# VectorE takes a group's residual behind the next group's locals, and TensorE turns x1 behind the cross matmuls

## The chip, the core and the metric

The kernel runs on one core of a Trainium2 chip. A core has five engines that work side by side, each with a queue of its own that it takes in order: TensorE (PE; its weight loads, PEld, overlap its matmuls), VectorE (DVE), ScalarE (ACT), GpSimd (POOL) and SyncE (SP, which issues the DMAs here). They wait for each other by semaphores. The metric is the time of one execution in device microseconds; the time of the kernel before is the median of three.

## The reference

32 batch rows of 128 tokens with 128 channels go through two layers, both with a residual. All is float32.

```python
# first layer (a gated trace layer), x: [32, 128, 128]
ctx    = causal_ema(x, tau_ctx)
wg     = sigmoid(concat([x, ctx]) @ Wg.T + bg)
gated  = x * wg
h1     = gelu(x @ Wn1.T + bn1)
mod    = 0.5 + sigmoid(h1 @ Wn2.T + bn2)                 # [b, t, 32]
traces = vmap(lambda tau, m: causal_ema(gated * m[..., None], tau))(tau_raws, mod)
temporal = einsum('dbtc,dc->btc', traces, softmax(blend, axis=0))
gate   = sigmoid(temporal @ Wtemp.T + btemp)
soma   = gelu(x @ Wsoma.T + bsoma)
out    = (soma * gate) @ Wout.T
x1     = x + (out - mean(out)) / sqrt(var(out) + 1e-5) * gamma + beta
# second layer: attention of 16 heads over 128 tokens; each batch row takes a dense or a
# sparse form by a threshold on exp(-5 * u_prev), then the output projection
q, k, v = x1 @ Wq.T + bq, x1 @ Wk.T + bk, x1 @ Wv.T + bv
y = x1 + attention(q, k, v, prior_indices, prior_mask, lam) @ Wo.T + bo
```

## The kernel before, in words

The 32 batch rows are 8 groups of 4 (`GB`); a group's tiles are 128 x 512. The first layer is a pipeline over the groups, in which every engine runs the same `step(i, m)`: it opens group m + 1 (functions `f_*`: context, gate, modulation, the eight lag products), finishes the traces of group m (`b_*`: carries, locals, cross, gate, output, moments) and closes group m - 1 (`c_*`: residual, q, k, v). There are seven steps; three are written out and four run in a loop of two turns, and all but the first close a group, so six do. After them `end()` works off the last group among the first attention rows, and `over_octets` does the attention (softmax over scores, two halves of 8 heads a batch row).

The order in each queue is written by hand. What matters around the change:

- VectorE: `b_carries` (three L1156, from PSUM to `bh`), `c_residual` of group m - 1 (four L1215: x1 = centred output times rstd plus xb), `f_gated` of group m + 1 (L1114, waits for ScalarE's tanh), `b_locals` (four L1165), `f_modulation` (L1120, L1121, L1124, L1126, L1128: the modulation and its split into bfloat16 parts `mod_pa` and `mod_pb`, each in SBUF), `b_temporal` (L1172, needs the turned cross), then the lag products (L1140, seven of L1144), with the rest of groups m and m - 1 between them.
- TensorE: local matmuls (L504, need the carries), `f_modulation` (L436), `c_x1T` (four transposes of x1, L385), `f_gated` (four transposes of the gated x, L385 too), `b_cross` (L515, need VectorE's locals), `f_modulation_n` (L446), `c_q` (L554, needs x1T on SBUF), `b_crossT` (L385, needs ScalarE's copy of cross), `c_k` (L557), then the lag matmuls (L470, L471; the first pair needs `mod_part3`, which VectorE's L1128 sets).
- ScalarE: the tanh of the gate (L811), of the modulation (L821), the copies of x1T (L854), of the turned gated x (L834), of cross (L839) and of the small modulation (L826).
- GpSimd: `f_inputs` of group m + 1 (L1386: xb = x + beta, waits for x1 of group m - 1), `c_keep` of m - 1 (L1418: x1 + bo), the decay products (L1393: three, then one; they need L826), the sums of lag products (L1406) and rstd (L1412). A load of x on SyncE's queue waits for xb.

`arena` is one large SBUF tensor that holds nearly all tiles; `ps` is PSUM. A row of the profile that reads `arena<-arena` has its tile operands in SBUF, one that reads `arena<-ps,arena` has one in PSUM.

Of the kernel before, what the change touches and what calls it, by code (L numbers as in the profile page):

```python
# [82 lines left out]
def build(nc, x, w, wn2, cols, rows, consts, ident_in, idx, masks, out):  # L83
    with ExitStack() as ctx:
# [156 lines left out]
        def at_start(i, m, before):  # L241

            return isinstance(i, int) and 2 * i + m < before
# [128 lines left out]
        def _(pe):  # L372
# [56 lines left out]
            def f_modulation(i, m):  # L429

                u = m % 2
                pe.wait_ge(s["h1_ready"], grp(i, m, 1, 1))
                if at_start(i, m, 1):
                    pe.wait_ge(s["vec_step"], vec(f"wn2_row{GB - 1}"))
                for b in range(GB):
                    mm = pe.matmul(bank(u, 1)[:, b * P:b * P + P], wn2_row[:, b, :], h1T[u], start=True, stop=True)  # L436
                mm.then_inc(s["modT_ps"], 1)
# [11 lines left out]
            def f_gated(i, m):  # L449

                u = m % 2
                pe.wait_ge(s["gated_ready"], grp(i, m, 1, 1))
                turned(bank(u, 2), gT[u], "gn_ps")
# [54 lines left out]
            def b_cross(i, m):  # L508

                u = m % 2  # L510
                pe.wait_ge(s["bh_ready"], grp(i, m, NJ + NCAR, NJ + NCAR))
                for j in range(NJ):

                    k = P if j else NLOC * D
                    mm = pe.matmul(bank(u, 0)[D * j:D * j + D, :], decay_p[0:k, :], bh[u][0:k, j, :],  # L515
                                   start=True, stop=True)
                mm.then_inc(s["cross_ps"], 1)
# [74 lines left out]
            def step(i, m):  # L592
                f_x(i, m + 1)
                f_context(i, m + 1)
                b_carries(i, m)
                f_soma(i, m + 1)
                f_gate(i, m + 1)
                f_hidden(i, m + 1)
                b_locals(i, m)
                f_modulation(i, m + 1)  # L600
                if not at_start(i, m, 1):
                    c_x1T(i, m - 1)
                f_gated(i, m + 1)
                b_cross(i, m)
                f_modulation_n(i, m + 1)
                if not at_start(i, m, 1):
                    c_q(i, m - 1)
                b_crossT(i, m)
                if not at_start(i, m, 1):
                    c_k(i, m - 1)  # L610
                f_lags(i, m + 1, range(0, 2))
                if not at_start(i, m, 1):
                    c_less(i, m - 1, 0, 0)
                b_gate(i, m)
                if not at_start(i, m, 1):
                    c_less(i, m - 1, 1, 0)
                f_lags(i, m + 1, range(2, 4))
                if not at_start(i, m, 1):
                    c_less(i, m - 1, 0, 1)
                f_lags(i, m + 1, range(4, 6))  # L620
                if not at_start(i, m, 1):
                    c_less(i, m - 1, 1, 1)
                    c_v(i, m - 1)
                b_out(i, m)
                f_lags(i, m + 1, range(6, Q))
                if at_start(i, m, 1):

                    pe.wait_ge(s["vec_step"], vec(f"hot{K_SPARSE - 1}"))
                    for j in range(K_SPARSE):
                        mm = pe.matmul(bank(1, 3)[:, 0:P], ident_b[:], one_hot[:, j, :],  # L630
                                       start=(j == 0), stop=(j == K_SPARSE - 1))
                    mm.then_inc(s["counts_ps"], 1)
# [147 lines left out]
        def _(act):  # L780
# [37 lines left out]
            def f_modulation(i, m):  # L818
                u = m % 2
                act.wait_ge(s["modT_ps"], grp(i, m, 1, 1))  # L820
                act.activation(thd[u], bank(u, 1), ACT.Tanh, bias=hb[:, 2:3], scale=0.5).then_inc(s["modT_tanh"], 1)  # L821
# [9 lines left out]
            def f_gated(i, m):  # L831
                u = m % 2
                act.wait_ge(s["gn_ps"], grp(i, m, 1, 1))
                act.activation(gn[u], bank(u, 2), ACT.Copy).then_inc(s["gn_ready"], 1)  # L834

            def b_cross(i, m):
                u = m % 2
                act.wait_ge(s["cross_ps"], grp(i, m, 1, 1))
                act.activation(crn[u], bank(u, 0), ACT.Copy).then_inc(s["cross_ready"], 1)  # L839
# [57 lines left out]
            def step(i, m):  # L897
                f_x(i, m + 1)
                f_context(i, m + 1)
                f_soma(i, m + 1)  # L900
                f_gate(i, m + 1)
                f_hidden(i, m + 1)
                f_modulation(i, m + 1)
                if not at_start(i, m, 1):
                    c_x1T(i, m - 1)
                f_gated(i, m + 1)
                b_cross(i, m)
                f_modulation_n(i, m + 1)
                if not at_start(i, m, 1):
                    c_parts(i, m - 1, 0)  # L910
                    c_part(i, m - 1, 0, 1)
                b_gate(i, m)
                if not at_start(i, m, 1):
                    c_part(i, m - 1, 1, 1)
                    c_parts(i, m - 1, 2)
                if at_start(i, m, 2) and m == 1:

                    act.wait_ge(s["vec_step"], vec("cnt_one"))
                    act.activation(lncnt[:], cnt1[:], ACT.Ln).then_inc(s["lncnt_ready"], 1)
# [85 lines left out]
        def _(dve):  # L1005
# [153 lines left out]
            def b_locals(i, m):  # L1159

                u = m % 2
                dve.wait_ge(s["local_ps"], grp(i, m, 1, 1))
                rows_of = slice(0, NLOC * D)
                for j in range(NJ):
                    dve.tensor_tensor(by_row(bh[u][rows_of, j, :]), by_row(bank(u, j)[rows_of, :]),  # L1165
                                      each_row_of(rows_of), ALU.mult).then_inc(s["bh_ready"], 1)
# [37 lines left out]
            def c_residual(i, m):  # L1204

                u = m % 2
                dve.wait_ge(s["rstd_ready"], grp(i, m, 1, 1))
                dve.wait_ge(s["xb_ready"], grp(i, m, 1, 1))
                dve.wait_ge(s["centred"], grp(i, m, GB, GB))
                if not at_start(i, m, 2):  # L1210

                    dve.wait_ge(s["x1b_ready"], grp(i, m, 1, 0))
                for b in range(GB):
                    cs = slice(b * P, b * P + P)
                    ins = dve.scalar_tensor_tensor(x1g[u][:, cs], ln[u][:, cs], rstd[:, u, b:b + 1], xb[u][:, cs],  # L1215
                                                   ALU.mult, ALU.add)
                ins.then_inc(s["x1_ready"], 1)
# [15 lines left out]
            def step(i, m):  # L1233
                closes, counts = not at_start(i, m, 1), at_start(i, m, 1)
                b_carries(i, m)
                if closes:
                    c_residual(i, m - 1)
                if counts:
                    neighbours()
                    one_hots(0, 8)  # L1240
                f_gated(i, m + 1)
                b_locals(i, m)
                if counts:
                    one_hots(8, 12)
                f_modulation(i, m + 1)
                b_temporal(i, m)
                if counts:
                    one_hots(12, 16)
                f_lags(i, m + 1, range(0, 2))
                if counts:  # L1250
                    one_hots(16, 20)
                f_lags(i, m + 1, range(2, 3))
                if counts:
                    one_hots(20, 24)
                f_lags(i, m + 1, range(3, 4))
                if counts:
                    one_hots(24, 28)
                b_mixed(i, m)
                f_lags(i, m + 1, range(4, 5))
                if counts:  # L1260
                    one_hots(28, K_SPARSE)
                f_lags(i, m + 1, range(5, 6))
                if closes:
                    c_values(i, m - 1)
                f_lags(i, m + 1, range(6, 7))
                c_moments(i, m)
                f_lags(i, m + 1, range(7, Q))
                c_centre(i, m)
                if counts:
                    late_tables()  # L1270
                if at_start(i, m, 2) and m == 1:

                    dve.wait_ge(s["lncnt_ready"], 1)
                    dve.tensor_tensor(neg_lc[:], count_none[:], lncnt[:], ALU.subtract).then_inc(s["neg_lc_ready"], 1)
# [274 lines left out]
```

## Time and profile before

| | us |
|---|---|
| median of three executions | 354.29 |
| lowest, highest | 354.13, 356.16 |
| profiled execution, whole | 355.99 |
| its span | 354.2 |

| engine | busy us | share of the span |
|---|---|---|
| PE | 316.7 | 89% |
| PEld | 216.5 | 61% |
| DVE | 293.7 | 83% |
| POOL | 232.6 | 66% |
| ACT | 212.5 | 60% |

The span runs from the first to the last instruction of the profiled execution; its whole time has 1.8 us around it. Busy shares are means over the two stages. In the views that follow, "idle before" is the time for which an engine stood still in front of an instruction, with what released it; where it stands at 0 or is missing the engine came straight from other work.

### The profile page before, as it was taken

The numbers are of one execution on the slowest core, as the hardware profiler recorded it, in microseconds if no ns is written. First come the engines' busy times: TensorE is split into PE (matmuls) and PEld (weight loads), VectorE is DVE, ScalarE is ACT, GpSimd is POOL, SyncE is SP. The second block draws the span as 40 slices with busy tenths as digits, with TensorE's granted clock in tenths as the row PEclk, the third lists the DMA queues.
The fourth block names the chain that finished last, engine by engine and source line by source line (L and its number), as shares of the span: only waits on it lengthen the run. The fifth ranks groups of instructions, "written<-read, shape, count | busy, mean of one in ns | idle before, by whom it ended". The sixth has DMA issues, their size and how long they took to land. (4 is left out here: it accounts for less than half of the span.)

```text
span 354.2 us, 10381 instructions
## 1 busy us (share of the span) xinstructions
PE 316.7 (89%) x3371; PEld 216.5 (61%) x3383; DVE 293.7 (83%) x1530; ACT 212.5 (60%) x452; POOL 232.6 (66%) x281
## 2 busy tenths in 40 slices
PE   1859579999898989899897989899999999999995
PEld 0515227557375655557453676677777777777774
DVE  4775997869788796968789976799999999999982
ACT  5743210475635455463631857778888888888873
POOL 3045054275555737454574877799999999999990
PEclk9989766999999999999999989999999999999999
DMA  7101000100100025500255045444444444301011
GB/s 218 43 0 32 0 0 2 31 4 0 31 0 30 3 59 78 73 0 0 42 70 70 2 65 98 118 124 91 114 107 126 100 115 97 94 3 32 5 31 31
DMA packets 23489, 18.91 MB, mean 53 GB/s; under 512 B 2320, under 2 KB 23056, under 8 KB 23440
## 3 DMA queue, kind: packets, MB, share of 16 engines
q1 hardware_dynamic: 23440, 18.31, 23.9%
q8 instruction: 25, 0.41, 0.5%
q14 instruction: 24, 0.20, 0.2%
HBM read 3.62 MB, written 2.10 MB: 16 GB/s over the span
## 5 line engine op out<-in xcount | busy, mean ns | idle before, releaser
L1446 POOL TENSOR_TENSOR arena<-arena,neg_max 128x512 f32<-128x512 f32 x128 | 130.4, 1064 | 14.2 <-DVE neg_max L1316 14.0
L1316 DVE CUSTOM_DVE_ANT_0 arena<-ps,arena 128x128 f32<-128x128 f32 x512 | 113.6, 286 | 8.6 <-issue 5.4
L963 ACT ACTIVATE arena<-ps 128x512 f32<-128x512 f32 x128 | 69.6, 597 | 9.3 <-PE ps L691 9.2
L691 PE MATMUL ps<-ident_sb,arena 128*128 128x128 f32 x512 | 69.0, 278 | 0.0
L691 PEld LDWEIGHTS ps<-ident_sb,arena 128*128 128x128 f32 x512 | 57.1, 142 | 7.0 <-POOL arena L1446 3.8
L1406 POOL TENSOR_TENSOR arena<-arena 128x448 f32<-128x448 f32 (+6 forms) x56 | 39.9, 713 | 31.1 <-DVE arena L1144 28.9
L1393 POOL TENSOR_TENSOR arena<-decay_a,arena 128x192 f32<-128x192 f32 x32 | 22.1, 712 | 40.9 <-ACT arena L826 40.9
L1316 DVE DVE_READ_ACCUMULATOR2_ANT neg_max<- 128x1 f32 x512 | 42.4, 83 | 0.1
L707 PE MATMUL ps<-arena 128*32 128x128 f32 x1024 | 41.2, 279 | 0.0
L1144 DVE TENSOR_TENSOR arena<-ps,arena 128x448 f32<-128x448 f32 (+6 forms) x56 | 23.6, 428 | 17.1 <-PE ps L471 10.0
L707 PEld LDWEIGHTS ps<-arena 128*32 128x32 f32 x1024 | 24.1, 109 | 6.9 <-issue 0.3
L677 PE MATMUL ps<-arena 48*128 48x128 bf16 x512 | 25.4, 219 | 2.9 <-DVE neg_max L1316 2.9
L385 PE MATMUL ps<-ident_sb,arena 128*128 128x128 f32 x128 | 19.5, 285 | 8.7 <-DMA arena<-in_x 5.7
L471 PE MATMUL ps<-mod_pb,lag_b 128*128 128x512 bf16 x64 | 26.4, 413 | 0.8 <-issue 0.4
L470 PE MATMUL ps<-mod_pa,lag_a 128*128 128x512 bf16 x56 | 23.4, 417 | 4.1 <-DVE arena L1144 2.5
L1386 POOL TENSOR_TENSOR arena<-arena,rows_sb 128x512 f32<-128x512 f32 x8 | 10.2, 1274 | 24.9 <-DVE arena L1215 21.2
L970 ACT ACTIVATE arena<-ps 128x256 f32<-128x256 f32 x32 | 12.3, 385 | 19.5 <-PE ps L707 19.5
L385 PEld LDWEIGHTS ps<-ident_sb,arena 128*128 128x128 f32 x128 | 15.4, 146 | 13.8 <-DMA ident_sb<-in_ident 5.6
L677 PEld LDWEIGHTS ps<-arena 48*128 48x128 bf16 x512 | 14.4, 94 | 15.4 <-DVE neg_max L1316 9.6
L794 ACT ACTIVATE arena<-ps 128x512 f32<-128x512 f32 x8 | 4.8, 595 | 29.6 <-PE ps L385 29.6
L861 ACT ACTIVATE k_parts<-ps,hb 128x512 bf16<-128x512 f32 (+1 forms) x24 | 16.5, 688 | 7.3 <-PE ps L557 3.8
L1165 DVE TENSOR_TENSOR arena<-ps,half_bw 96x512 f32<-96x512 f32 x32 | 19.8, 678 | 0.4 <-PE ps L504 0.4
(156 smaller groups left out, 602.6 us busy)
## 6 DMA issues: line engine op xcount, KB each, us to landing
arena<-q_parts SPq DMA_DIRECT2D x96, 64.0 KB
arena<-k_parts SPq DMA_DIRECT2D x96, 64.0 KB
arena<-in_x SPq DMA_DIRECT2D x8, 256.0 KB, 2.7
out<-arena SPq DMA_DIRECT2D x7, 256.0 KB, 3.1
w_sb<-in_w SPq DMA_DIRECT2D x1, 576.0 KB, 6.4
arena<-in_consts SPq DMA_DIRECT2D x1, 420.0 KB, 4.1
rows_sb<-in_rows SPq DMA_DIRECT2D x1, 288.5 KB, 3.0
out<-arena SPq DMA_DIRECT2D x1, 192.0 KB, 2.0
```

Source lines behind the costliest of these rows:

```text
L385: mm = pe.transpose(out_bank[:, cs], src[:, cs], ident)
L470: pe.matmul(bank(u, lag % 2), lag_a[:, lag, :], mod_pa[u][:], start=True, stop=False)
L471: pe.matmul(bank(u, lag % 2), lag_b[:, lag, :], mod_pb[u][:], start=False, stop=True)\
L677: mm = pe.matmul(ps[0][:, score_bank(c) + slot, k * P:k * P + P], q_stack[rows_of, 4 * o + k, b * P:b * P + P], k_stack[rows_of, 4 * o + k ...
L691: mm = pe.transpose(ps[1][:, q % 2, k * P:k * P + P], neg_t[q % NT_RING][:, k * P:k * P + P], ident)
L707: mm = pe.matmul(ps[1][D * k:D * k + D, 2, o * P:o * P + P], vx[n % 2][:, v0:v0 + D], probT[(2 * c + slot) % PT_RING][:, k * P:k * P + P], ...
L963: act.activation(probT[q % PT_RING], ps[1][:, q % 2, :], ACT.Exp, scale=-1.0)\
L1144: dve.tensor_tensor(packed(prod[u][lag % 2], lag), chunks(bank(u, lag % 2), 0, Q - lag), chunks(gT[u], 0, Q - lag), ALU.mult).then_inc(s[" ...
L1316: dve.tensor_tensor_reduce(out=neg_t[q % NT_RING][:, cs], in0=ps[0][:, score_bank(c) + slot, cs], in1=nbias[n % 2], scale=1.0, scalar=3.0e ...
L1393: pool.tensor_tensor(mod_a[u][:, b * W:b * W + ND * D].rearrange("p (k d) -> p k d", d=D), decay_a[:], modn[u][:, b * D:b * D + D].unsquee ...
L1406: pool.tensor_tensor(a, a, pr_, ALU.add).then_inc(s["lag_added"], 1)
L1446: pool.tensor_tensor(t4, t4, neg_max[:, n % 2, 4 * z:4 * z + 4].unsqueeze(2).broadcast_to([P, 4, P]), ALU.subtract).then_inc(s["shifted"], 1)
```

## The change

Nothing is added or removed. On VectorE `c_residual` of group m - 1 moves from in front of `f_gated` to behind `b_locals`. On TensorE `c_x1T` of group m - 1 moves from in front of `f_gated` to behind `b_cross`, and ScalarE's copy of x1T moves in the same way.

```diff
--- TensorE, step(i, m)
                 b_locals(i, m)
                 f_modulation(i, m + 1)
+                f_gated(i, m + 1)
+                b_cross(i, m)
                 if not at_start(i, m, 1):
                     c_x1T(i, m - 1)
-                f_gated(i, m + 1)
-                b_cross(i, m)
                 f_modulation_n(i, m + 1)
                 if not at_start(i, m, 1):
                     c_q(i, m - 1)
--- ScalarE, step(i, m)
                 f_modulation(i, m + 1)
+                f_gated(i, m + 1)
+                b_cross(i, m)
                 if not at_start(i, m, 1):
                     c_x1T(i, m - 1)
-                f_gated(i, m + 1)
-                b_cross(i, m)
                 f_modulation_n(i, m + 1)
--- VectorE, step(i, m)
                 b_carries(i, m)
-                if closes:
-                    c_residual(i, m - 1)
                 if counts:
                     neighbours()
                     one_hots(0, 8)
                 f_gated(i, m + 1)
                 b_locals(i, m)
+                if closes:
+                    c_residual(i, m - 1)
                 if counts:
                     one_hots(8, 12)
                 f_modulation(i, m + 1)
```

On VectorE, in the first step that closes a group, the piece of the queue from the carries to the modulation reads so (- before, + after; L1215 is the residual, L1114 the gate product, L1165 the locals, L1120 the first modulation instruction):

```order
 L1156 TENSOR_TENSOR arena<-ps,half_bw 32x512 x3
-L1215 SCALAR_TENSOR_TENSOR arena<-arena,rstd 128x128 x4
 L1114 SCALAR_TENSOR_TENSOR arena<-ps,arena 128x512
 L1165 TENSOR_TENSOR arena<-ps,half_bw 96x512 x4
+L1215 SCALAR_TENSOR_TENSOR arena<-arena,rstd 128x128 x4
 L1120 TENSOR_SCALAR arena<-arena 128x512
 L1121 TENSOR_SCALAR mod_pa<-arena 128x512
```

The four residuals stand behind the gate product and the four locals now, directly ahead of the modulation.

On TensorE, in the same step, from the local matmuls to q (L385 x8 is the turn of x1 and that of the gated x together, L515 the cross matmuls, L554 is q):

```order
 L504 MATMUL ps<-arena 96x128 x16
 L436 MATMUL ps<-arena,wn_row 128x128 x4
-L385 MATMUL ps<-ident_sb,arena 128x128 x8
+L385 MATMUL ps<-ident_sb,arena 128x128 x4
 L515 MATMUL ps<-arena,decay_p 32x512 x4
+L385 MATMUL ps<-ident_sb,arena 128x128 x4
 L446 MATMUL ps<-ident_sb,arena 128x32 x4
 L554 MATMUL ps<-arena,w_sb 128x512
```

Four of the eight transposes, those of x1, stand behind the cross matmuls, two places ahead of q, which needs their copy.

## Rows read from the trace of the kernel before

**Rows 1.** Busy time by stretch: stretch, length, then engines (instructions), TensorE's clock, DMA.

```profile
60.60:181.90 121.30, 114.75 (x845) 70.73 (x850) 98.20 (x240) 67.96 (x117) 65.67 (x82) 1.00 0.16 28
205.00:354.00 149.00, 143.69 (x2155) 113.29 (x2156) 128.38 (x1047) 113.08 (x281) 133.26 (x150) 0.99 0.34 80
```

**Rows 2.** Order of time on VectorE in one step: start, length, instruction, idle before.

```profile
125.55 1.14 DVE L1215 SCALAR_TENSOR_TENSOR arena<-arena,rstd 128x128 f32<-128x128 f32 x4
126.72 0.69 DVE L1114 SCALAR_TENSOR_TENSOR arena<-ps,arena 128x512 f32<-128x512 f32 x1
127.33 2.47 DVE L1165 TENSOR_TENSOR arena<-ps,half_bw 96x512 f32<-96x512 f32 x4
129.72 0.41 DVE L1120 TENSOR_SCALAR arena<-arena 128x512 f32<-128x512 f32 x1
...
131.30 0.42 DVE L1126 CAST mod_pa<-arena 64x512 bf16<-64x512 f32 x1
131.76 0.69 DVE L1128 TENSOR_TENSOR mod_pb<-arena,mod_pa 32x512 bf16<-32x512 f32 x1
132.88 0.69 DVE L1172 TENSOR_TENSOR arena<-ps,arena 128x512 f32<-128x512 f32 x1 [0.42 <-PE ps L385]
134.10 0.69 DVE L1140 TENSOR_TENSOR arena<-ps,arena 128x512 f32<-128x512 f32 x1 [0.53 <-PE ps L471]
```

**Rows 3.** The same step on TensorE.

```profile
125.61 1.13 PE L504 MATMUL ps<-arena 32*96 32x128 f32 x32
...
129.85 1.06 PE L515 MATMUL ps<-arena,decay_p 96*32 96x512 f32 x8 [1.15 <-DVE arena L1165]
...
131.21 1.13 PE L554 MATMUL ps<-arena,w_sb 128*128 128x512 f32 x2
132.17 0.60 PE L385 MATMUL ps<-ident_sb,arena 128*128 128x128 f32 x4
...
133.68 0.38 PE L471 MATMUL ps<-mod_pb,lag_b 128*128 128x512 bf16 x1
...
131.74 0.14 PEld L385 LDWEIGHTS ps<-ident_sb,arena 128*128 128x128 f32 x1 [0.24 <-ACT arena L839]
```

**Rows 4.** The same step on ScalarE.

```profile
125.36 0.66 ACT L811 ACTIVATE ps<-ps,hb 128x512 f32<-128x512 f32 x1 [1.03 <-PE ps L415]
...
128.46 0.59 ACT L854 ACTIVATE arena<-ps 128x512 f32<-128x512 f32 x1
...
130.99 0.60 ACT L839 ACTIVATE arena<-ps 128x512 f32<-128x512 f32 x1 [1.46 <-PE ps L515]
```

**Rows 5.** The same step on GpSimd; L1393 is the first of three.

```profile
126.77 1.27 POOL L1386 TENSOR_TENSOR arena<-arena,rows_sb 128x512 f32<-128x512 f32 x1 [2.96 <-DVE arena L1215]
128.01 1.27 POOL L1418 TENSOR_TENSOR x1b_all<-arena,rows_sb 128x512 f32 x1
...
131.83 1.08 POOL L1393 TENSOR_TENSOR arena<-decay_a,arena 128x192 f32<-128x192 f32 x1 [2.55 <-ACT arena L826]
```

**Rows 6.** Durations of L1085 and L1393 (min/median/max), then instructions beside each other.

```profile
L1085 DVE TENSOR_SCALAR arena<-key_no,idx_m x32: 270/276/1111, 36.3 to 55.5; 128x128 bf16<-128x128 f32 x32
L1393 POOL TENSOR_TENSOR arena<-decay_a,arena x32: 579/601/1079, 21.0 to 180.2; 128x192 f32<-128x192 f32 x32
54.24 0.73 POOL L1406 TENSOR_TENSOR arena<-arena 128x256 f32<-128x256 f32 x1 [1.48 <-DVE arena L1144]
54.28 0.77 DVE L1085 TENSOR_SCALAR arena<-key_no,idx_m 128x128 bf16<-128x128 f32 x1
54.93 0.59 POOL L1393 TENSOR_TENSOR arena<-decay_a,arena 128x192 f32<-128x192 f32 x1
54.98 0.63 DVE L1085 TENSOR_SCALAR arena<-key_no,idx_m 128x128 bf16<-128x128 f32 x1
191.05 1.14 POOL L1446 TENSOR_TENSOR arena<-arena,neg_max 128x512 f32<-128x512 f32 x1 [2.65 <-DVE neg_max L1316]
191.15 1.18 DVE L1215 SCALAR_TENSOR_TENSOR arena<-arena,rstd 128x128 f32<-128x128 f32 x1
```

## The prediction

> **What bounds the kernel now.** I read the busy time by stretch first [rows 1]. The program has two stages. Six steps that carry three groups at a time fill 60.6 to 181.9 us (121.3 us, 20.2 us a step), and the attention over 32 batch rows fills 205 to the end. The change touches only the six steps, so I leave the 149 us of attention as they are: nothing is moved in them, and what stands between 181.9 and 205 is in the old order too. In the six steps TensorE is busy for 114.75 of 121.3 us, VectorE for 98.2, ScalarE for 68.0 and GpSimd for 65.7.
>
> Busy shares don't say what sets the step's length, so I read one step in order of time on each engine [rows 2 to 5]. The chain through it is this. VectorE comes straight from the carries (L1156) and at 125.55 begins the four residuals of the closing group (L1215, 1.14 us), the gate product (L1114) and the four locals (L1165), which end at 129.80. TensorE's cross matmuls (L515) wait for that last local (1.15 us idle) and start at 129.85; ScalarE copies them out (L839, 130.99 to 131.59), TensorE turns the copy (L385 at 132.17), and VectorE adds it (L1172, at 132.88, after 0.42 us of waiting). From there TensorE runs without a gap into the lag matmuls, and VectorE's first lag product (L1140) follows at 134.10. The rest of the step hangs on that product. So the stretch 125.5 to 134.1 is where a moved instruction can count. The five modulation instructions on VectorE (L1120 to L1128, 129.72 to 132.45) end ahead of the turned copy and are hidden now by 0.43 us. GpSimd is idle for 2.96 us until x1 is there, then makes the next xb (L1386) and keeps x1 (L1418), ending at 129.28 [rows 5].
>
> **The change, part by part.** No instruction is added or removed; 4 residuals, 4 transposes (with their copy on ScalarE) go to other places in each of six steps.
>
> *What the residual's move frees.* The gate product need not wait for 1.14 us of residual, but it needs ScalarE's tanh (L811), which ends at 125.36 + 0.66 = 126.02 [rows 4]; with some 0.06 us of handover it runs 126.08 to 126.77. TensorE's local matmuls end at 125.61 + 1.13 = 126.74 [rows 3], so the locals run 126.80 to 129.27, ahead of the old 129.80 by 0.53 us. Cross matmuls: 129.32 instead of 129.85. So of 1.14 us only 0.53 is freed.
>
> *The turn of x1.* The residual now follows the locals and ends at 129.27 - 0.08 + 1.14 = 130.33 (successive instructions overlap by 0.08, as 127.33 + 2.47 against 129.72). The transposes of x1 start at about 130.38; they take 0.60 us and some 0.13 to be handed on, so their copy (L854, 0.59 us) runs 131.11 to 131.70, and q (L554), which needs it, starts at 131.85 (0.15 us from ScalarE's end to TensorE, as L839 to L385). Before it started at 131.21. The turned cross stands behind q in TensorE's queue: it and L1172 come 0.64 us later, at 133.52. So even the freed 0.53 is lost, for q stands ahead of what it would speed. This term alone is 6 x 0.64 = 3.8 us.
>
> *What x1 releases on GpSimd.* This is the large term. L1386 and L1418 need x1. Today they run from 126.77 to 129.28, beside L1114 and L1165, each of which has one operand in PSUM (`arena<-ps,...`), and neither side is stretched. After the change x1 arrives at 130.33, and the same 2.5 us fall on the modulation, whose five instructions have all their operands in SBUF. The rows show what happens to such pairs [rows 6]. A one-hot instruction (L1085, 0.27 us as a rule) took 0.77 us where GpSimd's L1406 ran, and up to 1.11; it ended 0.08 us behind GpSimd. A residual of 0.35 us took 1.18 us beside L1446, and ended 0.15 us behind it. The other way round, GpSimd's decay product (L1393, 0.60 us) took 1.08 us where VectorE's L1128 was under way (131.76 to 132.45). It ended 0.46 us behind L1128, as if it had begun 0.14 us before L1128's end. So the two take turns, and who comes second waits. They also alternate: at 54.93 GpSimd went from one instruction to the next, and a waiting L1085 got through in between; the next L1085 then took 0.63.
>
> With these handovers I walk both queues. A held VectorE instruction of 128 elements ended 0.08 us (L1085) or 0.15 us (L1215) behind GpSimd. For 512 elements that is at most four times as much, 0.33 and 0.58, and at least the duration less the 0.19 that L1085 has in front of its 0.08: 0.23 for L1126 and its like L1121, 0.50 for L1124 and L1128. I take the middle, 0.28 and 0.55, as an estimate. A held GpSimd instruction ends at VectorE's end - 0.14 + its own time. L1120 runs 130.24 to 130.66. GpSimd asks at 130.40: L1386 to 131.79. L1121 to 132.07. L1418 to 133.20. L1124 to 133.75. First L1393 to 134.21. L1126 to 134.49. Second L1393 to 134.95. L1128 to 135.50. Before, L1128 ended at 132.45: 3.05 us later. It is the last part of the modulation that the first lag matmul needs (L470 to L471, part 3). TensorE, idle by then, needs 0.05 + 0.10 + 0.22 us to start the second of the two, and VectorE follows 0.42 behind it (133.68 to 134.10), so the first product (L1140) starts at 136.29 instead of 134.10. L1172, behind L1128 on VectorE, is done by 136.22 and fits in front. **2.19 us a step.** It contains the 0.64 of the turn, which is hidden beneath it. Behind this point TensorE, VectorE and ScalarE have the same work in the same order and shift together. GpSimd has its third decay product done at 135.96, and its first sum (L1406) needs a product that VectorE makes only behind L1140.
>
> *Other things that move.* The next load of x waits for xb, 3.7 us later than now; its data is used a step later, so it stays hidden. ScalarE's copies change places and have idle time around them (1.46 us ahead of L839) [rows 4]. If that cover went, a copy's 0.6 us would come in. The clock granted is 1.00 of full speed in the six steps [rows 1], the 2.4 GHz level; I cost no change of it.
>
> **Sum.** 6 x 2.19 = 13.1 us. The profiled execution took 355.99 us, of which 354.2 is its span; with the term it would be 369.1. The median of the runs shown is 354.29, 1.7 below the profiled one, so the forecast is 354.29 + 13.1 = 367.4, say **367.3 us**.
>
> Bounds per step. If VectorE's L1121 gets through before GpSimd's first instruction, L1128 ends about 0.4 us earlier: 1.8 us a step, 365.1. If the handovers cost up to 0.3 more in sum, or TensorE's wait breaks the overlap of later work, 2.7 a step: 370.5. The forecast's own range is 363.5 to 371.5.
>
> **A rule weighed.** The row shows GpSimd beginning in effect 0.14 us before VectorE's instruction has ended (L1393 against L1128) [rows 5, 6]. The Trainium skill, page "SBUF — State Buffer", section "Who interferes with whom", says that the shared pair of SBUF ports is held for a whole instruction, and the second engine is blocked fully; its section "A bandwidth-pool intuition that's wrong" gives "blocked until DVE-end + ~115 ns" for a GpSimd-side wait. By that figure each of the four handovers to GpSimd would be 0.26 us dearer and the time 373.6 us. My sum goes by the trace's handover.
>
> **The rivals.**
> - *Only the turn of x1 counts* (0.12). GpSimd's work might find the gaps, or pause without holding VectorE. Then the step grows by 0.64: 354.29 + 3.8 = 358.1 us. For it: L1386 and L1418 aren't stretched today. Against: their partners today read PSUM, and every pair with all operands in SBUF in [rows 6] is stretched.
> - *Dearer handovers, or GpSimd keeps its turn* (0.07). If VectorE gets nothing through until all of GpSimd's five instructions have run, L1121 ends at 135.0 and L1128 at 136.9: 3.6 us a step, 376. Handovers that start only behind VectorE's end lie between this and the forecast. Against: the L1085 that got through at 54.97, and the 0.14 us by which L1393 began ahead. The rule of the page named above is a case of this rival.
> - *Faster* (0.02). The locals' 0.53 us reaches the turned cross in each step: 354.29 - 3.2 = 351.1 us. It decides for this if x1's copy is ready before the cross matmuls leave TensorE (130.3), so that q doesn't wait, and the modulation isn't held. The residual is done only at 130.33, so it can't be, unless the handovers are far shorter than in the rows.
> - *No change beyond 1%, by partial cover* (0.04): the 0.64 and 0.53 cancel in part, say 355 to 357.
> - *The forecast* (0.75).
>
> **How the numbers follow.** About 1% (3.5 us) is what a measurement of this kernel can tell from no change. The range takes the forecast's own and reaches down to the turn-only case and to its lower part: 357 to 372, leaving out the dear handovers, the faster case and tails of the others (under 0.2). Faster by over 1%: 0.02. Within 1%, which holds the partial case and some of the turn-only one (358.1 is just outside 357.8): 0.09. Slower: 0.89.
>
> **What the changed profile would show.** Right: L1386 at about 130.4 of such a step, directly beside the modulation; the modulation's instructions L1121, L1124, L1126, L1128 with means of 1.0 to 1.5 us instead of 0.42 and 0.69 (L1124 as L1128); VectorE's busy time up by 2.5 to 3 us a step, though its instructions are the same; a wait of TensorE's L470 for L1128 of some 2 us, which isn't there now; the locals' end 0.5 us nearer to the carries; steps of 22.4 us. L1172 would no longer wait for TensorE. Wrong: modulation durations unchanged and a step longer by 0.6 us, with TensorE's q waiting for L854 (then only the turn counts). Also wrong: waits of the attention stage changed, or a lower granted clock in the steps.

## The result

| | before | changed |
|---|---|---|
| median, us | 354.38 | 365.81 |
| lowest to highest, us | 354.13 to 356.16 | 364.43 to 367.24 |
| span of the profiled execution, us | 354.2 | 365.4 |

The changed kernel is slower. The ratio to before is 1.0308, with a 95% interval of 1.0269 to 1.0348: 11.4 us more in the medians, 11.2 us in the spans. The forecast was 367.3 us in a range of 357 to 372. (The median before is over four executions here, 354.29 was over three.)

The busy times of the same two stretches come first (stretch, length, busy time and instructions of TensorE, its weight loads, VectorE, ScalarE and GpSimd, then the granted clock). The six steps now fill some ten us more; the attention is as it was, TensorE's 143.69 us included [rows 1].

```profile
60.60:192.00 131.40, 115.77 (x831) 68.86 (x831) 110.28 (x237) 67.95 (x116) 70.56 (x82) 1.00 0.14 27
216.00:365.00 149.00, 143.69 (x2156) 113.14 (x2156) 128.77 (x1050) 113.08 (x281) 133.57 (x150) 0.99 0.37 80
```

VectorE's busy time grew by 12.1 us in the steps, GpSimd's by 4.9, for the same instructions. The changed kernel's VectorE in order of time, in the step that answers to [rows 2] (start, length, instruction, idle before):

```profile
130.94 0.69 DVE L1156 TENSOR_TENSOR arena<-ps,half_bw 32x512 f32<-32x512 f32 x1
132.25 0.69 DVE L1114 SCALAR_TENSOR_TENSOR arena<-ps,arena 128x512 f32<-128x512 f32 x1 [0.61 <-ACT ps L811]
132.92 2.48 DVE L1165 TENSOR_TENSOR arena<-ps,half_bw 96x512 f32<-96x512 f32 x4
135.32 1.13 DVE L1215 SCALAR_TENSOR_TENSOR arena<-arena,rstd 128x128 f32<-128x128 f32 x4
136.37 0.42 DVE L1120 TENSOR_SCALAR arena<-arena 128x512 f32<-128x512 f32 x1
136.71 0.42 DVE L1121 TENSOR_SCALAR mod_pa<-arena 128x512 bf16<-128x512 f32 x1
137.23 1.57 DVE L1124 TENSOR_TENSOR arena<-arena,mod_pa 128x512 f32<-128x512 f32 x1
138.83 1.39 DVE L1126 CAST mod_pa<-arena 64x512 bf16<-64x512 f32 x1
140.25 0.96 DVE L1128 TENSOR_TENSOR mod_pb<-arena,mod_pa 32x512 bf16<-32x512 f32 x1
141.25 0.69 DVE L1172 TENSOR_TENSOR arena<-ps,arena 128x512 f32<-128x512 f32 x1
141.95 0.69 DVE L1140 TENSOR_TENSOR arena<-ps,arena 128x512 f32<-128x512 f32 x1
```

And GpSimd beside it, which answers to [rows 5]:

```profile
136.53 1.72 POOL L1386 TENSOR_TENSOR arena<-arena,rows_sb 128x512 f32<-128x512 f32 x1 [6.60 <-DVE arena L1215]
138.21 1.72 POOL L1418 TENSOR_TENSOR x1b_all<-arena,rows_sb 128x512 f32 x1
139.90 2.33 POOL L1393 TENSOR_TENSOR arena<-decay_a,arena 128x192 f32<-128x192 f32 x3
```

The two tables interlock. L1386 asks at 136.53 and ends at 138.25; L1124, issued at 137.23, ends at 138.80. L1418 ends at 139.93; L1126 at 140.22. L1128 is held by the first decay product. Three instructions that took 0.69, 0.42 and 0.69 us [rows 2] take 1.57, 1.39 and 0.96. L1172 and L1140 follow without a gap, so VectorE now sets this stretch. TensorE waits ahead of L554 and L470, where it did not before; ahead of cross it stands idle for about as long as before (1.08 against 1.15 us) (start, length, instruction, idle before):

```profile
135.46 1.07 PE L515 MATMUL ps<-arena,decay_p 96*32 96x512 f32 x8 [1.08 <-DVE arena L1165]
136.50 0.66 PE L385 MATMUL ps<-ident_sb,arena 128*128 128x128 f32 x4
137.94 1.10 PE L554 MATMUL ps<-arena,w_sb 128*128 128x512 f32 x2 [0.42 <-ACT arena L854]
138.87 0.60 PE L385 MATMUL ps<-ident_sb,arena 128*128 128x128 f32 x4
139.31 1.02 PE L557 MATMUL ps<-arena,w_sb 128*128 128x512 f32 x2
141.32 0.38 PE L470 MATMUL ps<-mod_pa,lag_a 128*128 128x512 bf16 x1 [0.98 <-issue]
```

The 0.98 us ahead of L470 are put down to "issue", but the program has the wait there for part 3 of the modulation, and L470 starts 0.11 us behind L1128's end (141.21).

### The profile page after: what moved, and what is told of

Same layout as the page of the kernel before. It is cut to its first block and busy times, and to the rows that moved or that the text cites. A ratio compares the mean times of both kernels' runs of the same rounds, so it can differ in the third digit from the quotient of the medians.

```text
span 365.4 us, 10393 instructions
## 1 busy us (share of the span) xinstructions
PE 317.7 (87%) x3383; PEld 214.5 (59%) x3383; DVE 306.8 (84%) x1530; ACT 213.1 (58%) x452; POOL 238.6 (65%) x281
## 5 line engine op out<-in xcount | busy, mean ns | idle before, releaser
L1446 POOL TENSOR_TENSOR arena<-arena,neg_max 128x512 f32<-128x512 f32 x128 | 130.1, 1054 | 14.1 <-DVE neg_max L1316 13.9
L691 PE MATMUL ps<-ident_sb,arena 128*128 128x128 f32 x512 | 68.6, 277 | 0.0
L1386 POOL TENSOR_TENSOR arena<-arena,rows_sb 128x512 f32<-128x512 f32 x8 | 12.7, 1581 | 47.4 <-DVE arena L1215 43.6
L1393 POOL TENSOR_TENSOR arena<-decay_a,arena 128x192 f32<-128x192 f32 x32 | 23.2, 747 | 25.3 <-ACT arena L826 25.3
L470 PE MATMUL ps<-mod_pa,lag_a 128*128 128x512 bf16 x64 | 26.6, 415 | 10.6 <-issue 5.8
L385 PE MATMUL ps<-ident_sb,arena 128*128 128x128 f32 x128 | 21.2, 292 | 8.9 <-DMA arena<-in_x 5.8
L385 PEld LDWEIGHTS ps<-ident_sb,arena 128*128 128x128 f32 x128 | 15.6, 148 | 19.3 <-DVE arena L1215 5.9
L471 PE MATMUL ps<-mod_pb,lag_b 128*128 128x512 bf16 x64 | 26.3, 411 | 0.0
L470 PEld LDWEIGHTS ps<-mod_pa,lag_a 128*128 128x128 bf16 x64 | 6.4, 101 | 31.5 <-DVE arena L1144 14.8
L861 ACT ACTIVATE q_parts<-ps,hb 128x512 bf16<-128x512 f32 (+1 forms) x24 | 16.5, 689 | 14.2 <-PE ps L566 9.2
```

What stands on the lines that cost most here:

```text
L385: mm = pe.transpose(out_bank[:, cs], src[:, cs], ident)
L470: pe.matmul(bank(u, lag % 2), lag_a[:, lag, :], mod_pa[u][:], start=True, stop=False)
L471: pe.matmul(bank(u, lag % 2), lag_b[:, lag, :], mod_pb[u][:], start=False, stop=True)\
L691: mm = pe.transpose(ps[1][:, q % 2, k * P:k * P + P], neg_t[q % NT_RING][:, k * P:k * P + P], ident)
L1393: pool.tensor_tensor(mod_a[u][:, b * W:b * W + ND * D].rearrange("p (k d) -> p k d", d=D), decay_a[:], modn[u][:, b * D:b * D + D].unsquee ...
L1446: pool.tensor_tensor(t4, t4, neg_max[:, n % 2, 4 * z:4 * z + 4].unsqueeze(2).broadcast_to([P, 4, P]), ALU.subtract).then_inc(s["shifted"], 1)
```

## Theories

- **A.** GpSimd's instructions and the modulation hold each other because all their operands are in SBUF; what x1 releases beside the modulation is the loss.
- **B.** The turn of x1, and q behind it, are the loss; the stretched modulation is hidden.
- **C.** VectorE's own 1.14 us of residual ahead of the modulation is the loss.

A good measure for all kernels is the gate product on VectorE, which runs once in each of the six closing steps: the difference of its first and last start, divided by five, gives the step. It is 20.22 us before and 21.98 in the changed kernel (min/median/max in ns, first and last start; before, then changed):

```profile
L1114 DVE SCALAR_TENSOR_TENSOR arena<-ps,arena x6: 690/692/693, 66.2 to 167.3; 128x512 f32<-128x512 f32 x6
L1114 DVE SCALAR_TENSOR_TENSOR arena<-ps,arena x6: 690/691/692, 66.3 to 176.2; 128x512 f32<-128x512 f32 x6
```

## Experiments: where GpSimd's two instructions stand

**One of the two moved away.** The changed kernel, with this on GpSimd:

```diff
                 f_inputs(i, m + 1)
-                if not at_start(i, m, 1):
-                    c_keep(i, m - 1)
                 f_accumulate(i, m + 1)
                 c_rstd(i, m)
+                if not at_start(i, m, 1):
+                    c_keep(i, m - 1)
```

> The changed kernel, but GpSimd's c_keep (L1418) stands at the end of its step, behind rstd; L1386 stays directly behind x1. Theory A (GpSimd's instructions with operands in SBUF hold VectorE's modulation, one handover for each): one of the two large holds goes. L1121 passes, L1386 holds L1124, the decay products hold L1126 and L1128; the first lag product comes 1.0 us later than in the kernel before instead of 1.7: 354.4 + 6 x 1.0 = 360.4 us (359 to 362). VectorE's L1126 falls from 1.39 us to about 0.8. Theory B (the turn of x1 and q behind it set the step, the stretched modulation is hidden beneath): 365.8 as the changed kernel.

Measured: 361.23 us, ratio 1.0177 (1.0144 to 1.0209). The six instances each of L1124 and L1126 (min/median/max in ns, first and last start):

```profile
L1124 DVE TENSOR_TENSOR arena<-arena,mod_pa x6: 1567/1569/1575, 71.3 to 177.9; 128x512 f32<-128x512 f32 x6
L1126 DVE CAST mod_pa<-arena x6: 703/706/709, 72.9 to 179.5; 64x512 bf16<-64x512 f32 x6
```

L1126 fell from 1.39 to 0.71 us: it now waits for a decay product instead of for L1418. A step takes 21.3 us. One hold gone, 0.7 us a step back, 4.6 us in all.

**Both moved away.**

```diff
-                f_inputs(i, m + 1)
-                if not at_start(i, m, 1):
-                    c_keep(i, m - 1)
                 f_accumulate(i, m + 1)
                 c_rstd(i, m)
+                f_inputs(i, m + 1)
+                if not at_start(i, m, 1):
+                    c_keep(i, m - 1)
```

> The changed kernel, but GpSimd's f_inputs (L1386) and c_keep (L1418) both stand at the end of the step, where VectorE reads PSUM. Theory A: the modulation is back to about 2.7 us in all (L1124 0.69, L1126 0.42; perhaps one short hold by a decay product), and what is left is q behind the late x1T, 0.64 us a step: 354.4 + 3.8 = 358.2 us (357 to 359.5). Theory B (all of the loss is the turn and q): 365.8. Theory C (the 1.14 us of residual in front of the modulation are the loss by themselves, as VectorE's own work): about 354.4 + 6 x 1.1 = 361.

Measured: 360.33 us, 1.0144 (1.0117 to 1.017), above what A gave. The modulation is as A says (L1128 keeps a short hold by a decay product, 0.97 us), and the instances of L1124 and of the gate product:

```profile
L1124 DVE TENSOR_TENSOR arena<-arena,mod_pa x6: 692/692/694, 74.0 to 178.3; 128x512 f32<-128x512 f32 x6
L1114 DVE SCALAR_TENSOR_TENSOR arena<-ps,arena x6: 692/692/693, 69.0 to 173.3; 128x512 f32<-128x512 f32 x6
```

(173.3 - 69.0) / 5 = 20.86 us a step: 0.6 above before, as forecast. The rest is lost once, ahead of the first closing step's gate product. In the step before it, L1386 now meets VectorE's small tables. One of them, L1095, had taken 0.18 us; its one instance here:

```profile
L1095 DVE TENSOR_SCALAR not_use<-use_b x1: 1175/1175/1175, 60.8 to 60.8; 128x32 f32<-128x32 f32 x1
```

TensorE in order of time, directly behind it:

```profile
62.81 1.08 PE L491 MATMUL ps<-arena 128*96 128x128 f32 x8 [1.91 <-issue]
```

And the busy row of the 3.5 us that follow (the clock is the figure behind the instruction counts):

```profile
64.00:67.50 3.50, 3.50 (x5) 1.35 (x4) 2.06 (x3) 0.69 (x1) 0.00 (x0) 0.52 0.08 23
```

TensorE, which needs the last of these tables, sat idle for 1.91 us. For 1.2 us after that its granted clock was still 1.00, and from 64.0 on it was 0.52 of full speed for 3.5 us. Whether this was the excess was the next thing to try, with L1386 left in place in the step that closes nothing:

```diff
+                if at_start(i, m, 1):
+                    f_inputs(i, m + 1)
                 f_accumulate(i, m + 1)
                 c_rstd(i, m)
-                f_inputs(i, m + 1)
                 if not at_start(i, m, 1):
+                    f_inputs(i, m + 1)
                     c_keep(i, m - 1)
```

> As the kernel with both of GpSimd's instructions late, but the very first step, which closes no group, keeps L1386 in its old place. The 2.3 us that the first closing step lost there (VectorE's L1095 held by L1386, TensorE idle 1.9 us and then at half its clock) should go: steps of 20.84 us, 354.4 + 6 x 0.57 = 357.8 us (356.8 to 358.8). If that loss is not from L1386 in the first step: 360.3 again.

Measured: 358.97 us, 1.0151 (1.0115 to 1.0188) against a before of 354.08 in its runs. Its span was 356.7 us, against 360.6. The gate product:

```profile
L1114 DVE SCALAR_TENSOR_TENSOR arena<-ps,arena x6: 691/692/692, 64.9 to 169.2; 128x512 f32<-128x512 f32 x6
```

The same step, 20.86 us, and the first gate product comes 4.1 us earlier (64.9 against 69.0). The median lies 0.2 us above the interval that I had named. The size of the one-off loss isn't settled: by medians it is 1.4 us, with intervals of the two ratios that overlap, and by spans 3.9. Nor is all of the 4.1 us L1386's doing. TensorE's transposes (L385) ahead of that place already started 1.2 us apart in the two traces, at 59.40 and 58.23, before L1386 began at 60.66: matmuls that took 1.13 us in the later kernel's trace (L379, at 53.85) took 2.05 in the other's (at 54.34), where the granted clock between 53 and 58 us was 0.66 against 1.00. The edit touches nothing there.

B falls in its second half: the stretched modulation isn't hidden, for taking GpSimd's two instructions away returns 6.8 of 11.4 us, with VectorE's and TensorE's orders as in the changed kernel. What B says of the turn and q is left as the smaller part, 0.6 us a step. C needs more than the time, since 360.33 was nearer to its 361 than to A's 358.2. It would have left steps 1.1 us longer than before, 21.3 us, and they are 20.86; a later kernel takes another 0.44 off with VectorE's order unchanged.

**The holds alone, in the kernel before.** The orders of TensorE, VectorE and ScalarE are those of before; GpSimd starts the two instructions late:

```diff
             def step(i, m):
+                if not at_start(i, m, 1):
+                    pool.wait_ge(s["bh_ready"], grp(i, m, NJ + NCAR, NJ + NCAR))
                 f_inputs(i, m + 1)
```

> The kernel before with one wait more: in a closing step GpSimd's f_inputs and c_keep start only when VectorE's four locals are done, so they stand beside the modulation. TensorE's, VectorE's and ScalarE's orders are those of before. Theory A: L1386 holds L1124, L1418 holds L1126, the decay products hold L1128, which ends 2.1 us later; the first lag product comes 1.15 us later: 354.4 + 6.9 = 361.3 us (359.5 to 363). Theory B (no price for GpSimd's place): GpSimd had 1.4 us to spare ahead of its first sum, so 354.4, with L1124 at 0.69 us.

Measured: 363.26 us, 1.0249 (1.0218 to 1.0281), 0.3 us above A's range. GpSimd had 1.38 us of idle time ahead of its first sum, and it still has 1.58 with the delay, yet the delay costs 8.7 us. So GpSimd isn't late itself; it is what it holds. Its first sum before, and here in the first closing step:

```profile
135.40 1.06 POOL L1406 TENSOR_TENSOR arena<-arena 128x448 f32<-128x448 f32 x1 [1.38 <-DVE arena L1144]
75.81 1.06 POOL L1406 TENSOR_TENSOR arena<-arena 128x448 f32<-128x448 f32 x1 [1.58 <-DVE arena L1144]
```

The modulation's durations in the six steps:

```profile
L1121 DVE TENSOR_SCALAR mod_pa<-arena x6: 415/1496/1496, 68.9 to 177.2; 128x512 bf16<-128x512 f32 x6
L1124 DVE TENSOR_TENSOR arena<-arena,mod_pa x6: 1572/1574/1580, 70.5 to 178.8; 128x512 f32<-128x512 f32 x6
L1126 DVE CAST mod_pa<-arena x6: 706/708/1386, 72.1 to 180.4; 64x512 bf16<-64x512 f32 x6
```

Here both orders of handover that the prediction had weighed show up. In four steps L1386 got in between L1120 and L1121 (L1121 1.50 us, L1126 0.71), in two L1121 passed (0.42, then 1.38 for L1126). One step of each kind:

```profile
133.62 1.39 POOL L1386 TENSOR_TENSOR arena<-arena,rows_sb 128x512 f32<-128x512 f32 x1 [6.08 <-DVE arena L1165]
133.80 1.50 DVE L1121 TENSOR_SCALAR mod_pa<-arena 128x512 bf16<-128x512 f32 x1
112.35 0.41 DVE L1121 TENSOR_SCALAR mod_pa<-arena 128x512 bf16<-128x512 f32 x1
112.36 1.53 POOL L1386 TENSOR_TENSOR arena<-arena,rows_sb 128x512 f32<-128x512 f32 x1 [6.34 <-DVE arena L1165]
```

Within this execution the order is that of asking: L1121 starts 0.33 us behind L1120's start, and GpSimd asked 0.16 us behind it in the four steps and 0.35 in the two. In the changed kernel it asked 0.16 or 0.26 us behind, ahead of L1121, and L1121 passed all the same in all six steps. What makes the two kernels differ stays open.

That the place of the operands makes the hold is read from which pairs were stretched; no run moves an operand. It isn't the whole rule either. In the attention stage of the kernel before, VectorE's L1191, which reads and writes SBUF alone, ran beside GpSimd's L1446 (until 199.03) and took the same 0.38 us for four as at 58.15, where GpSimd was idle:

```profile
196.99 2.04 POOL L1446 TENSOR_TENSOR arena<-arena,neg_max 128x512 f32<-128x512 f32 x2 [0.56 <-DVE neg_max L1316]
198.70 0.38 DVE L1191 BATCH_NORM_AGGREGATE moments<-stats 128x2 f32<-128x6 f32 x4
```

## Experiments: the two moves apart

**The turn alone** (the parts of the change on TensorE and ScalarE; VectorE's order as before).

> Half of the change: x1T is turned and copied behind cross on TensorE and ScalarE, VectorE's residual stays in its old place. The transposes start behind the cross matmuls at 130.85 of the step shown, their copy ends at 132.15 behind that of cross, q starts at 132.3 instead of 131.2: 1.1 us a step, no instruction of VectorE or GpSimd longer: 354.4 + 6.5 = 360.9 us (358.5 to 362). If q's place does not matter (rival): 354.4. If the pair of moves only works together through GpSimd's holds: also 354.4, with L1124 at 0.69 us.

Measured: 361.25 us, 1.0167 (1.0122 to 1.0211). TensorE in one step:

```profile
133.40 1.06 PE L515 MATMUL ps<-arena,decay_p 96*32 96x512 f32 x8 [1.60 <-DVE arena L1165]
134.40 0.66 PE L385 MATMUL ps<-ident_sb,arena 128*128 128x128 f32 x4
...
135.84 1.10 PE L554 MATMUL ps<-arena,w_sb 128*128 128x512 f32 x2 [0.42 <-ACT arena L854]
```

From cross to q it is 2.44 us, against 1.36 [rows 3]. The transposes left the part of the step where TensorE stands idle anyway (1.60 us now, 1.15 before) and entered the full stretch behind cross, and q waits for their copy: 21.3 us a step. L1124 took 0.69 us in all steps.

**The residual alone** (the part on VectorE; TensorE's and ScalarE's orders as before).

> The other half of the change: VectorE's residual stands behind the locals, TensorE and ScalarE turn and copy x1T in their old places, ahead of the gated x and cross. Theory A: L1386 and L1418 start beside the modulation as in the changed kernel, L1128 ends at the same place, and L1172 and L1140 follow straight behind it; cross comes 0.6 us later than in the changed kernel, which is hidden under the stretched modulation: 365.8 us (364.5 to 367.5), steps of 22.0 us. Theory B (the place of the turn decides, the modulation does not): cross waits for x1, and q comes 1.6 us late: 354.4 + 9.8 = 364, with L1172 waiting for TensorE; the modulation's own waits tell the two apart.

Measured: 376.57 us, 1.0625 (1.0589 to 1.0661). Neither theory had this: it is 10.8 us slower than the whole change. TensorE in one step:

```profile
141.71 1.97 PE L385 MATMUL ps<-ident_sb,arena 128*128 128x128 f32 x8 [2.56 <-DVE arena L1215]
143.60 1.61 PE L515 MATMUL ps<-arena,decay_p 96*32 96x512 f32 x8
```

The busy row of the steps, with the granted clock behind the instruction counts:

```profile
62.00:195.00 133.00, 117.60 (x786) 69.61 (x785) 102.74 (x224) 62.81 (x104) 63.14 (x75) 0.90 0.11 22
```

With the transposes of x1 still first in TensorE's queue, the engine stands idle for 2.56 us until the late residual is done. After that the same eight transposes take 1.97 us and cross 1.61, while cross takes 1.06 at full speed [rows 3], and the mean granted clock of the steps is 0.90. Read in stretches of 2 us, it falls to 0.50 in each of the six steps (between 142 and 144 us in this one) and nowhere below 0.97 in the steps of the changed kernel. I formed a further theory: the idle time brings the clock down to its lower level (1.2 of 2.4 GHz) for a spell, and that is the price beyond A. The test adds work in the idle time:

```diff
                 if not at_start(i, m, 1):
+                    busy_while_waiting(i, m - 1)
                     c_x1T(i, m - 1)
...
+            def busy_while_waiting(i, m):
+                pe.wait_ge(s["h1_ready"], grp(i, m, 1, 3))
+                pe.wait_ge(s["centred"], grp(i, m, GB, GB))
+                for _ in range(10):
+                    pe.matmul(closing_bank(i, m, 3), lag_a[:, 0, :], mod_pa[(m + 1) % 2][:], start=True, stop=True)
```

> The kernel with VectorE's residual move alone (376.6 us measured), with ten matmuls more in each closing step whose results are not used (into a bank that the turn of x1 then overwrites). They fill 2.1 us in which TensorE waits for x1 there. Theory A2 (formed from that run: its 2.56 us of idle TensorE is followed by a stretch at half the clock, in which the transposes take 1.97 us instead of 1.04 and cross 1.61 instead of 1.06): with TensorE kept busy the granted clock stays at 1.00 in the steps, the transposes are back at about 1.04 and cross at 1.06, the step falls from 23.2 to 25.2 us to about 21.8, and the time to 354.4 + 6 x 1.6 = 364 us (362.5 to 367). If the order of the queues alone costs 22 us (rival), adding work changes nothing or makes it slower: 376 to 378.

Measured: 365.79 us, 1.0337 (1.0316 to 1.0357). TensorE in one step (L552 are the added matmuls, L1222 is the residual in this file):

```profile
133.09 2.10 PE L552 MATMUL ps<-mod_pa,lag_a 128*128 128x512 bf16 x9
135.59 1.09 PE L385 MATMUL ps<-ident_sb,arena 128*128 128x128 f32 x8 [0.40 <-DVE arena L1222]
136.62 1.06 PE L515 MATMUL ps<-arena,decay_p 96*32 96x512 f32 x8
```

The busy row of the steps:

```profile
62.00:195.00 133.00, 128.77 (x893) 75.33 (x906) 112.67 (x248) 67.38 (x115) 72.84 (x85) 1.00 0.15 27
```

Its gate product (L1121 in this file):

```profile
L1121 DVE SCALAR_TENSOR_TENSOR arena<-ps,arena x6: 691/692/693, 65.4 to 175.3; 128x512 f32<-128x512 f32 x6
```

Sixty useless matmuls made the kernel 10.8 us faster. The clock stays at 1.00, cross is back at 1.06. What is left is the time of the whole change, 365.8, and its step, 21.98 us: with the clock kept, the place of the turn makes no difference, since the stretched modulation covers it, as A had said. So in the whole change the turn's move buys back what the residual's move would have cost in clock.

## Experiments: what q's place costs, and a faster order

**q behind the turned cross.** The kernel with both of GpSimd's instructions late from the first closing step, and on TensorE:

```diff
-                if not at_start(i, m, 1):
-                    c_q(i, m - 1)
                 b_crossT(i, m)
                 if not at_start(i, m, 1):
+                    c_q(i, m - 1)
                     c_k(i, m - 1)
```

> The changed kernel with GpSimd's L1386 and L1418 at the end of each closing step, and TensorE's q (L554) behind the turned cross (L385) instead of ahead of it. Theory A: with the holds gone and q no longer in front, L1172 comes about where it was, TensorE has the transposes of x1 in a full stretch instead of an idle one (0.54 us) and cross 0.53 us earlier, which cancel: L1140 0.1 to 0.2 us later than before, 354.4 + 0.9 = 355.3 us (354 to 357). If q's place ahead of the turned cross is not what costs 0.57 a step (rival), the time is that of the next kernel, 357.8.

Measured: 356.84 us, 1.0069 (1.0041 to 1.0096), 2.1 below the same kernel with q in front. The gate product (one line higher in this file) runs from 66.2 to 168.3, that is 20.42 us a step:

```profile
L1113 DVE SCALAR_TENSOR_TENSOR arena<-ps,arena x6: 691/692/692, 66.2 to 168.3; 128x512 f32<-128x512 f32 x6
```

So 0.44 of the 0.6 us left a step was q's wait. The freed 0.53 us of the locals is eaten by the four transposes in TensorE's full stretch: from the carries' end to cross it is 3.8 us instead of 4.3, from cross to the lag matmul L471 4.5 instead of 3.8. The step stays 0.2 us above before.

**k in TensorE's idle time.** This starts from the kernel before. The picture so far says that TensorE has 1.15 us idle ahead of cross [rows 3] and none from cross to the lag matmuls. k needs only x1T, so it can go there if x1 is turned a little sooner:

```diff
--- TensorE, step(i, m); ScalarE's c_x1T moves ahead of its f_modulation too
                 b_locals(i, m)
-                f_modulation(i, m + 1)
                 if not at_start(i, m, 1):
                     c_x1T(i, m - 1)
+                f_modulation(i, m + 1)
                 f_gated(i, m + 1)
+                if not at_start(i, m, 1):
+                    c_k(i, m - 1)
                 b_cross(i, m)
...
                 b_crossT(i, m)
-                if not at_start(i, m, 1):
-                    c_k(i, m - 1)
                 f_lags(i, m + 1, range(0, 2))
```

k is given the wait for x1T's copy that only q had before.

> The kernel before with TensorE's order changed another way: x1T is turned ahead of the modulation matmuls (ScalarE copies it there too), and k (L557) stands between the gated x and cross, in TensorE's idle 1.15 us, instead of behind the turned cross. VectorE and GpSimd as before. Theory A's picture (TensorE runs without a gap from cross to the lag matmuls, and has 1.15 us idle ahead of cross): k's 0.86 us leaves the full stretch; L1140 can start at L1172's end, 0.5 to 0.6 us earlier, a step of 19.5 to 19.8 us: 354.4 - 3.6 = 350.8 us (349 to 352.5). If VectorE's own work sets the step (rival), 354.4.

Measured: 349.33 us against 354.08, ratio 0.9877 (0.9849 to 0.9905): faster than both kernels. TensorE in one step (L558 is k here):

```profile
125.39 1.02 PE L558 MATMUL ps<-arena,w_sb 128*128 128x512 f32 x2
126.68 1.07 PE L515 MATMUL ps<-arena,decay_p 96*32 96x512 f32 x8 [0.26 <-DVE arena L1166]
129.00 0.60 PE L385 MATMUL ps<-ident_sb,arena 128*128 128x128 f32 x4
129.44 0.38 PE L470 MATMUL ps<-mod_pa,lag_a 128*128 128x512 bf16 x1
```

The gate product (L1115 in this file):

```profile
L1115 DVE SCALAR_TENSOR_TENSOR arena<-ps,arena x6: 692/692/693, 65.3 to 162.5; 128x512 f32<-128x512 f32 x6
```

The idle time ahead of cross fell from 1.15 to 0.26 us, and the lag matmuls start 0.44 us behind the turned cross. A step takes 19.44 us, 0.8 less than before. That VectorE's own work sets the step there is thereby ruled out.

## Why the prediction was right

Point by point, by its own steps:

- *Only 0.53 of the residual's 1.14 us is freed.* Right. The gate product waited 0.61 us for ScalarE's tanh; the locals ended 3.77 us behind the carries' end (131.63 to 135.40), against the 3.75 worked out.
- *The turn of x1, with the freed 0.53 lost behind q, is 0.64 us a step.* Right: with GpSimd's instructions away the step is 0.6 above before, and putting q behind the turned cross takes 0.44 of it back. In the changed kernel q started 6.3 us behind the carries' end, as forecast. (The turn by itself, without the residual's move, costs 1.1 us a step.)
- *GpSimd's two instructions fall on the modulation and hold it.* Right, and shown from both sides: removed from the changed kernel, put into the kernel before.
- *The handovers.* (Times behind the carries' end, 125.52 in the step before and 131.63 in the one after.) The mechanism held, the order was the other of the two bounded. I let L1386 in ahead of L1121; in the changed kernel L1121 passed in all six steps (0.41 to 0.42 us). L1128 ended at 9.58 us instead of 9.98, and L1140 started at 10.31 instead of 10.77. That is 1.73 us later a step than before (8.58), where the sum had 2.19; the lower bound was 1.8. This term, 6 x 0.46 = 2.8 us too much, is the mis-sized one. With the bound's order the sum gave 365.1.
- *The sum.* 6 x 1.73 = 10.4 of 11.2 us of span. The first lag product started 2.45 us later in the first closing step (73.57 to 76.02) and 11.28 later in the sixth (174.64 to 185.92), which is 1.77 a step from the first to the last. Of the first 2.45, 0.2 were there at the carries' end already (64.95 to 65.16), and the first closing step lost 0.5 more than the step shown; the prediction has neither. So the forecast of 367.3 was only 1.5 us high where its term was 2.8 too large, and that part is luck.
- *The signs.* The modulation was stretched, L1172 no longer waits for TensorE, and the locals end 0.5 us nearer to the carries. Their sizes were too large: L1121 wasn't held, VectorE's busy time grew by 2.0 us a step instead of 2.5 to 3, L470 waited for 0.98 us instead of some 2, and the step is 21.98 us instead of 22.4.
- *The held lengths.* For the 0.69 us kind I put the end 0.55 us behind GpSimd's; L1124 ended 0.55 behind L1386. For the 0.42 us kind 0.28; L1126 ended 0.29 behind L1418.
- *No change of the clock.* Right, at 1.00, but for a reason that the prediction didn't see: had the turn of x1 stayed in its place, the clock would have fallen.
- *The dearer handover.* The Trainium skill, page "SBUF — State Buffer", section "A bandwidth-pool intuition that's wrong", gives "blocked until DVE-end + ~115 ns" for the descriptors that GpSimd writes for a DMA. It isn't borne out for the instructions here: L1386 ended 1.13 us behind L1121's end with 1.27 us of its own, so it began in effect 0.14 us ahead of that end.

## What to carry to other kernels

When an instruction is moved, ask what it releases on the other engines and what those instructions will then stand beside: GpSimd's 2.5 us were free beside instructions that read PSUM and cost 1.4 us a step beside the modulation, which has all its operands in SBUF, though no queue had more work. Here a reordering paid where it filled an idle stretch of the engine that is full afterwards (k ahead of cross), and cost time where it took work out of one (the turn of x1, as long as x1 was early). Before moving what TensorE waits for, look at how long it will stand idle: the wait of 2.56 us a step was paid a second time in clock, waits up to 1.6 us a step were not.

## What the runs showed of the hardware beyond expectation

- TensorE idle for 2.56 us a step was followed by a stretch at the lower clock, in which eight transposes took 1.97 instead of 1.09 us; idle waits of 1.60 us (the turn alone), 1.15 (before) and 1.08 (the changed kernel) left the clock of the six steps at full speed, while the single wait of 1.91 us shown above was followed, 1.2 us after its end, by 3.5 us at 0.52. What separates them is not settled. Ten unused matmuls in the wait kept it up.
- In the changed kernel VectorE's modulation and GpSimd's instructions took turns, one each, with no gap at the handover (rows above: L1386, L1124, L1418, L1126, the first decay product, L1128). Whether GpSimd got in between L1120 and L1121 went by who asked first within one execution, but not from one kernel to the other.
